# Graph attention heads: prelu reads the source scores from two PSUM banks, and transposes and products share the other six

## What is computed

```python
h = x @ W                                   # (625, heads, c)
as_n = (h * a_src).sum(-1)                  # source scores, one per node and head
ad_n = (h * a_dst).sum(-1)                  # destination scores
e = leaky_relu(as_n[src] + ad_n[dst], 0.2)
m = segment_max(e, dst)
p = exp(e - m[dst])
s = segment_sum(p, dst)
out = segment_sum(p / s[dst] * h[src], dst) + b
```

## Time and profile before

| | |
|---|---|
| time of three runs, median (lowest, highest) | 2859.42 us (2855.84, 2861.07) |
| the profiled execution: its own time | 2858.89 us |
| its span | 2856.7 us |
| PE busy | 2709.0 us, 95% of the span |
| DVE busy | 1397.8 us, 49% |
| ACT busy | 1142.1 us, 40% |
| POOL busy | 710.3 us, 25% |

### The profile page before, as it was taken

How to read it: one execution, slowest core, us unless ns; L and a number is a source line. 1 busy time by engine, 2 the same in 40 slices (tenths; PEclk the granted TensorE clock), 3 DMA queues, 4 the chain that set the end, 5 groups by cost and what they waited for, 6 DMA issues and landing times. The chain is left out here.

```text
span 2856.7 us, 49216 instructions
## 1 busy us (share of the span) xinstructions
PE 2709.0 (95%) x20011; PEld 2466.1 (86%) x20011; DVE 1397.8 (49%) x3595; ACT 1142.1 (40%) x2131; POOL 710.3 (25%) x265
## 2 busy tenths in 40 slices
PE   9999999998688999998899999999998999999999
PEld 9999999995338978998897999999668897797799
DVE  9877475664122134558742552241664454302743
ACT  7633265561004203328631263332563432355431
POOL 0144311110002422220324343323204441114022
PEclk9999999999799999999999999999999999999999
DMA  2022231026992211221021222222001121111112
GB/s 67 14 76 81 86 98 40 29 84 234 413 383 74 63 39 46 67 83 41 12 89 39 67 68 78 78 67 78 29 1 46 61 71 41 60 34 35 34 45 72
DMA packets 169681, 223.22 MB, mean 78 GB/s; under 512 B 22051, under 2 KB 150719, under 8 KB 169208
## 3 DMA queue, kind: packets, MB, share of 16 engines
q1 hardware_dynamic: 169458, 220.07, 23.2%
HBM read 216.56 MB, written 3.48 MB: 77 GB/s over the span
## 5 line engine op out<-in xcount | busy, mean ns | idle before, releaser
L284 POOL TENSOR_TENSOR weights_r<-weights,head_weights_r 128x1536 fp32r<-128x1536 f32 (+1 forms) x78 | 278.7, 3573 | 1085.5 <-ACT head_weights_r L277 1075.6
L58 PE MATMUL ps<-weights_r,buf_r 128*125 128x256 f32 (+2 forms) x3794 | 510.6, 285 | 5.2 <-DVE kv L2989 1.7
L284 POOL TENSOR_TENSOR weights_r<-weights,weights_r 128x1536 fp32r<-128x1536 f32 (+1 forms) x74 | 262.4, 3546 | 907.7 <-ACT weights_r L277 907.7
L58 PEld LDWEIGHTS ps<-weights_r,buf_r 128*125 128x125 f32 x3794 | 478.0, 187 | 8.4 <-issue 3.5
L58 PE MATMUL ps<-head_weights_r,buf_r 128*125 128x256 f32 (+3 forms) x2548 | 350.7, 284 | 0.0
L58 PE MATMUL ps<-xT_r,weights_r 128*128 128x376 f32 (+3 forms) x2016 | 330.3, 309 | 0.0
L58 PEld LDWEIGHTS ps<-head_weights_r,buf_r 128*125 128x125 f32 (+1 forms) x2548 | 325.1, 187 | 0.0
L58 PEld LDWEIGHTS ps<-xT_r,weights_r 128*128 128x128 f32 x2016 | 304.7, 191 | 0.0
L58 PE MATMUL ps<-weights_r,xT_r 128*125 128x256 f32 x1680 | 231.5, 282 | 1.7 <-DVE resid L2400 0.9
L277 ACT ACTIVATE head_weights_r<-weights 128x1536 fp32r<-128x1536 f32 (+1 forms) x78 | 115.9, 1486 | 268.9 <-PE ps L58 158.1
L58 PEld LDWEIGHTS ps<-weights_r,xT_r 128*125 128x125 f32 x1680 | 211.9, 186 | 3.2 <-PE ps L2331 1.5
(11 more groups left out here) (420 smaller groups left out, 4339.8 us busy)
## 6 DMA issues: line engine op xcount, KB each, us to landing
expert_regions<-in_L_ffn_w SPq DMA_DIRECT2D x64, 576.0 KB, 12.7
expert_regions<-in_L_ffn_w SPq DMA_DIRECT2D x36, 768.0 KB, 20.4
weights<-in_L_mix_fc_w SPq DMA_DIRECT2D x24, 768.0 KB, 4.4
weights<-in_L_gnn_W SPq DMA_DIRECT2D x18, 768.0 KB, 4.5
expert_regions<-in_L_ffn_w SPq DMA_DIRECT2D x24, 384.0 KB, 9.5
weights<-in_L_ffn_W SPq DMA_DIRECT2D x11, 768.0 KB, 4.8
weights<-in_L_mix_w_mapT SPq DMA_DIRECT2D x9, 768.0 KB, 4.7
weights<-in_L_gnn_W_out SPq DMA_DIRECT2D x9, 768.0 KB, 4.5
```

What stands on the lines that cost most here:

```text
L58: mm = net.nc.tensor.matmul(ps, net.r(stationary(s, k)), net.r(moving(m, k)), start=(n == 0 and k == 0), stop=(stop and n == 2 and k == kc ...
L284: self.nc.gpsimd.tensor_tensor(self.r(load.dst), load.dst, self.r(load.high), ALU.subtract).then_inc(self.low_made, 1)
```

## The change

Each head but the first of an attention gets its row without a copy: prelu reads the two PSUM banks directly, as one stretch of 625 columns (`direct`). The banks 6 and 7 are kept for rows within such a stage, and turns and products go round the other six (`banks`). Eight bank numbers are taken from the program's ring for the stage, and at its end each of the eight is free when its last reader is done (`held`). The row of head k+1 now stands on PE ahead of turns(k), in the same stage; the first head's row keeps its place and its two copies. The banks of a direct row are free when leaky 4 of its head is done. Stages of a single head have no direct row, but their turns and products go round six banks as well.

```diff
 class GatHeads(Heads):
+    ROWS = BANKS - 2
+    held = ()
...
         n = k + 1
-        ahead = n + 1 < len(self.heads)
         if k < 0 and self.begun is None:
             pe += [("row", n, j) for j in range(2)]
             act += [("row", n, j) for j in range(2)]
+        if apply and scores:
+            pe += [("row", n, j) for j in range(2)]
         if apply:
             turns = [("turn", k, s, j) for j in range(2) for s in range(NT)]
             pe += turns
...
-        if scores and ahead:
-            pe += [("row", n + 1, j) for j in range(2)]
         if apply:
             pe += [("apply", k, t, j) for t in range(NT) for j in range(self.nw)]
...
                 if t + 1 < NT:
                     act.append(("leaky", n, t + 1))
-                elif ahead:
-                    act += [("row", n + 1, j) for j in range(2)]
                 act.append(("exp", n, t))
...
+    def banks(self):
+
+        net = self.net
+        if not any(q[0] == "apply" for q in self.order["pe"]):
+            return super().banks()
+        ring = [net.bank() for _ in range(BANKS)]
+        held = {b % BANKS: net.freed[b - BANKS] for b in ring}
+        bank, self.prior, turn = {}, {}, 0
+        for q in self.order["pe"]:
+            if q[0] == "row":
+                b = self.ROWS + q[2]
+            else:
+                b, turn = turn % self.ROWS, turn + 1
+            bank[q], self.prior[q] = b, held[b]
+            engine, entry = self.reader(q)
+            held[b] = ({"act": net.act, "dve": net.dve}[engine].sem, self.at[engine][entry])
+        self.held = [(b, held[b % BANKS]) for b in ring]
+        return bank
+
+    def direct(self, k):
+
+        w = (HALVES[0][1] - HALVES[0][0]) * TP
+        return self.net.ps[:TP, self.ROWS:self.ROWS + 2, :].rearrange("p b c -> p (b c)")[:, 512 - w:512 - w + N]
...
-                ins = nc.scalar.activation(self.P[k % 2][:, t], self.net.asb[:TP, :], ACT.Prelu, bias=self.heads[k][1][:, t:t + 1], scale=-SLOPE, alpha=1.0 / SLOPE)
+                ins = nc.scalar.activation(self.P[k % 2][:, t], self.direct(k) if k > 0 else self.net.asb[:TP, :], ACT.Prelu, bias=self.heads[k][1][:, t:t + 1], scale=-SLOPE, alpha=1.0 / SLOPE)
```

More of the change, by code:

```diff
@@ L2189 @@
 class Heads(Stage):
+    prior = None
     def schedule(self, n_heads, first, prior):
@@ L2207, in schedule @@
         self.bank = self.banks()
-        for q, b in self.bank.items():
+        for q, b in self.bank.items() if not self.prior else ():
             engine, entry = self.reader(q)
@@ L2259, in __init__ @@
             self.at[e].update(begun.at[e])
+        for b, mark in self.held:
+            net.freed[b] = mark
         if first >= 0:
@@ L2303, in step, with wait_bank @@
         dve += outs
+    def banks(self):
[15 more added lines that the diff above has]
+        return bank
+    def wait_bank(self, pe, q):
+        if self.prior:
+            pe.wait_ge(*self.prior[q])
+        else:
+            super().wait_bank(pe, q)
+    def direct(self, k):
+        w = (HALVES[0][1] - HALVES[0][0]) * TP
+        return self.net.ps[:TP, self.ROWS:self.ROWS + 2, :].rearrange("p b c -> p (b c)")[:, 512 - w:512 - w + N]
     def reader(self, q):
-        return {"row": ("act", q), "turn": (self.turn_engine(*q[2:]) if q[0] == "turn" else "", q), "apply": ("dve", ("out",) + q[1:])}[q[0]]
+        return {"row": ("act", ("leaky", q[1], NT - 1) if q[1] > 0 else q), "turn": (self.turn_engine(*q[2:]) if q[0] == "turn" else "", q), "apply": ("dve", ("out",) + q[1:])}[q[0]]
     def tensor(self, pe):
@@ L2315, in tensor @@
                 t0, t1 = HALVES[q[2]]
-                ps = self.ps(q, TP, (t1 - t0) * TP)
+                ps = self.direct(k)[:, t0 * TP:t1 * TP] if k > 0 else self.ps(q, TP, (t1 - t0) * TP)
                 for t in range(t0, t1):
@@ L2342, in scalar @@
                 self.wait(act, "pe", *q)
-                if k > 0 and q[2] == 0:
-                    self.wait(act, "act", "leaky", k - 1, NT - 1)
                 ins = nc.scalar.activation(self.net.asb[:TP, t0 * TP:t1 * TP], self.ps(q, TP, (t1 - t0) * TP), ACT.Identity)
@@ L2352, in scalar @@
                 if t == 0:
-                    self.wait(act, "act", "row", k, 1)
+                    self.wait(act, *(("pe", "row", k, 1) if k > 0 else ("act", "row", k, 1)))
                     if k > 1:
                         self.wait(act, "pe", "turn", k - 2, NT - 1, 1)
-                ins = nc.scalar.activation(self.P[k % 2][:, t], self.net.asb[:TP, :], ACT.Prelu, bias=self.heads[k][1][:, t:t + 1], scale=-SLOPE, alpha=1.0 / SLOPE)
+                ins = nc.scalar.activation(self.P[k % 2][:, t], self.direct(k) if k > 0 else self.net.asb[:TP, :], ACT.Prelu, bias=self.heads[k][1][:, t:t + 1], scale=-SLOPE, alpha=1.0 / SLOPE)
             else:
```

## The result

| | median | lowest to highest | runs |
|---|---|---|---|
| before | 2860.00 us | 2854.66 to 2861.99 | 8 |
| changed | 2863.98 us | 2860.54 to 2868.92 | 8 |

The ratio is 1.0023, 95% interval 1.0015 to 1.0032. Against 2859.42 us, to which the forecast of 2864.5 was tied, the changed kernel's median is 4.6 us more. The changed kernel's profiled execution took 2864.97 us (span 2862.8), that of before 2858.89 (span 2856.7): 6.1 us between the two traces.

The account below looks back on a forecast made before the run. In the eight heads a loop through ACT and DVE was taken as the bound, in four-head attentions mostly PE. Terms 2.9 + 2.4 + 0.1 - 0.3 = +5.1 us on 2859.42 gave 2864.5 us, range 2857.5 to 2869.5.

Parts of the forecast that it names:

- Copies on ACT: In 16 heads, 32 copies totalling 11.7 us go from ACT; covered by DVE's order, so 0 gained.
- Prelu from PSUM: Only leaky 0 is on the path, in about 14 heads; prelu 0.02 us shorter each, -0.3 us.
- Ring of six: Eight-head attention: turn 5 waits for the previous head's last eviction, 0.43 us in each of 7 heads, +2.9 us.
- Four-head attentions: Second and third: the same wait costs 0.35, 0.35 and 0.52 us by head, 1.2 us each, +2.4 us.
- The first: First four-head attention: DVE starts late and a row fills the gap; -0.65, +0.28 and +0.44 give +0.1 us.
- Single heads: Single-head stages: no head ahead whose last eviction could be awaited, and longer products; 0.
- Moved rows: Second head's row enters the attention's stage, costing 1.09 us of PE and returning 1.09 where it stood; 0, four times.
- The rival of a low clock in every head: Eight heads: added waiting drops PE's clock to 1.2 GHz, 7 us over the loop per head, +50 us; chance 0.02.

Follow-up runs that it names:

- x4: Changed kernel with the 32 ACT copies back ahead of exp 4, their result not used; median 2861.83 us, ratio 1.0017 to before.
- x9: x7 with the 32 ACT copies back ahead of exp 4, their result not used; median 2849.09 us, ratio 0.9966 to before.
- x8: Kernel before, eight banks and copies kept, with ACT doing leaky 0 and 1 ahead of the evictions of j = 1; 2849.48 us, ratio 0.9962.
- x3: Kernel before with only the ring of six: transposes and products on six banks, rows on the other two, copies kept; 2863.05 us, ratio 1.0020.
- x1: Changed kernel with a head's last `out` placed ahead of sum and rinv on DVE; 2858.73 us, ratio 1.0005 to before.
- x2: Changed kernel, six banks, with the bank of a head's last product given to turn 9 instead of turn 5; 2857.47 us, ratio 0.9996.
- x5: Changed kernel with the direct row moved between the transposes of j = 0 and those of j = 1; 2865.62 us, ratio 1.0020.
- x7: x2 with ACT doing leaky 0 and 1 ahead of the evictions of j = 1; 2844.24 us, ratio 0.9947 to before.
- x12: x7 unchanged, timed again; 2845.41 us, ratio 0.9962 to before.
- x10: Changed kernel unchanged, timed again; 2864.16 us, ratio 1.0020 to before.

## Why the prediction was right

Forecast 2864.5 us, range 2857.5 to 2869.5; measured 2863.98. Sum forecast 5.1 us; the traces show 4.9 in the attentions of several heads and 0.4 more in a single head, for which the forecast had nothing. That the median came within 0.5 us is luck in part: a dip of the clock is a quarter of the sum, and what lies outside the attentions, where the forecast wanted no difference, came to 0.8 us between the two traces. By its steps:

- **Copies on ACT, 0.** Shown by x4, and by x9 where ACT is full. The count was off: forecast was 11.7 us of ACT's busy time, 9.5 went. In x8 a pair stands 0.62 us apart from what follows (1337.97 to 1338.59), since an instruction's row overlaps the next one's; 16 x 0.62 is 9.9. I had summed lengths where starts count. With the copies back, x4 has 10.9 us more of busy time; the three sizes aren't brought to one here.
- **Prelu from PSUM, 0.78 us, -0.3.** 773 ns for one group of 30 and 786 for 50, against 812 and 815 before (means). The Trainium skill (ScalarE: Activation LUTs, "What ACT_TABLE_LOAD costs") gives 801 for 625 columns, an estimate from its two figures, whatever the source; here PSUM is some 30 ns below SBUF, and the measurement decides.
- **Ring of six, 2.9.** Shown by x3, x1 and x2. Ten transposes end 2.06 us behind count 4 (1339.45 less 1337.39), before 1.63 (1336.10 less 1334.47): 0.43, the forecast size, but two errors of 0.1 us cancel in it. The start moved by 0.56, not 0.66: the handover behind `out` is 0.06 us, not the 0.15 behind count. And the ten transposes take 1.19 us (1338.10 to 1339.29), not the 1.09 of ten that follow without a wait: behind a wait the second one starts 0.21 us after the first, where the others stand 0.11 apart. Seven times 0.43 is 3.0 and not 2.9, a slip of the sum. The period grew by 0.40, since prelu is shorter; in x3, with prelu from SBUF, it grew by 0.43.
- **Four-head attentions, 1.2 each.** 1.0 each: 0.32, 0.23 and 0.41 for 0.35, 0.35 and 0.52. The sums of 11 us were good to 0.1 us, and the handover, shorter by 0.09 three times, is about the difference.
- **The first, +0.1.** Between -0.1 and +0.4 in two traces of the changed kernel: head 1 lost 1.24 and 1.68 us for 1.45 forecast. It hangs on a transfer: DVE started 1.64 and 2.07 us behind the first product, and 1.84 before, which by its sum the forecast kept.
- **Single heads, 0.** Wrong for the last one, by 0.4 us (above). The forecast asked only for the last eviction of a head ahead; it didn't ask for turns 6 to 9, which wait for ACT's evictions of the same head.
- **Moved rows, 0.** In each trace the linear layer starts 1.08 us earlier against its surroundings, and the attention is entered with the same wait:

```profile
452.66 0.94 PE L58 MATMUL ps<-weights_r,xT_r 128*125 128x256 f32 x6
...
535.01 1.32 PE L2350 MATMUL ps<-ident,stats 125*125 125x125 f32 x10 [0.60 <-DVE buf L2430]
536.17 2.95 PE L1755 MATMUL ps<-ident,buf 125*128 125x125 f32 x24
```

  Row 0 of the third attention waits 0.60 us for the last eviction, as forecast, and the 24 transposes behind it follow without the 0.84 us that they waited in the earlier trace rows: absorbed.
- **Not named:** turn 4 waits 0.19 us for the `out` before the last, and the row 0.80 for leaky 4. Both lie ahead of a wait that ends later, so the sum holds, but x5 was misjudged for want of the first.
- **The clock** stayed at 1.00 in the eight heads with PE busy for 75.35 of 90 us (77.26 in the earlier trace rows), and at 0.983 over the span, in both traces of the changed kernel. The rival of a low clock in every head would have given 50 us, and no trace shows it. The Trainium skill (TensorE: Matmul & The Clock Gate, "A second HAM failure mode: psum-queue depth-cycling") tells of a clock that goes up and down as PE cycles through PSUM banks and idles briefly between its groups; no trace here shows that head by head. What x1 and x5 show is one fall to half in one head, for some 7 and 3 us, so a small form of that rival was possible and had no place in the forecast. The kernel before had such a fall as well, which the prediction overlooked: in the single head at 2366 us, behind a wait of 3.55 us, the granted clock was 0.62, and 25 transposes took 4.42 us where the last single head's took 2.80.

## What to carry to other kernels

When buffers are taken out of a ring, ask for each wait which reader frees the buffer and where that reader stands in its engine's order; whether the ring is large enough on average says little. Here the last reader stood behind small work that it doesn't need (sum and rinv, 0.34 us), and a buffer that comes free late can go to the group that wants it late. Room made on an engine that is waited for by nobody is worth nothing until another order uses the idle time: here ACT's order alone gave 0.4%.

## Not expected of the hardware

PE takes up work 0.06 us behind an `out` of DVE and 0.15 us behind a count. A count has a second instruction of 0.08 us behind it, which stores its value (DVE_READ_ACCUMULATOR2 in the rows), but both end at 1337.39, so that alone doesn't explain the difference, and its cause isn't shown. And the granted clock dips, at a cost of 1.3 to 1.5 us, at a place of a linear layer in the trace of one kernel and not in that of another with the same work ahead of it, which by itself is a quarter of the difference that was to be measured. In x1 it was 2.7 us, inside the attention. The largest such difference lies behind the last attention, where no work was changed: from 2547 us to the end, x1, x3, x4, x7 and x12 gain 4.1 to 4.5 us on the kernel before, and the changed kernel, x2, x5, x9 and x10 less than 0.2 us. The 6.1 us between the two traces are free of it; the medians may not be, as the five runs of x12 fall into two groups of about that distance (2844.7 to 2845.4 and 2849.8 to 2850.4 us).
